# Gathers of both MoE layers in groups of four, with the landing of each group awaited at the next border

## The reference

```
h = layernorm(x) * (1 + ca) + sa;   x = x + ga * attention(h)
h = layernorm(x) * (1 + cb) + sb;   x = x + gb * ffn(h)
```

```
gate, up = split(routed_in @ gate_up);  routed = (up * silu(gate)) @ down
shared = silu(h @ Wg.T) * (h @ Wu.T) @ Wd.T;   ffn = shared + routed
```

## Time and profile before

| what | value |
| --- | --- |
| times of three runs | 1258.29, 1261.92, 1263.23 us |
| profiled execution, its own time | 1255.22 us |
| its span | 1253.4 us |
| PE busy | 1061.6 us, 85% of the span |
| DVE busy | 938.9 us, 75% |
| ACT busy | 780.5 us, 62% |
| POOL busy | 323.2 us, 26% |
| mean granted TensorE clock | 0.926 of full speed |

### The profile page before, as it was taken

The page is one execution under the profiler, slowest core; times in us unless marked ns, Lnnn a source line. Parts: engine busy times, 40 slices in busy tenths (PEclk is TensorE's granted clock), DMA queues, the critical chain, the costliest instruction groups (busy, mean ns, idle before and its releaser), DMA issues. The chain is left out here.

```text
span 1253.4 us, 23783 instructions
## 1 busy us (share of the span) xinstructions
PE 1061.6 (85%) x9052; PEld 507.1 (40%) x9052; DVE 938.9 (75%) x1445; ACT 780.5 (62%) x1539; POOL 323.2 (26%) x464
## 2 busy tenths in 40 slices
PE   6886789577779999999999999999998997179737
PEld 4785689433302222222222222222222974157315
DVE  7976244477799999999999999999990873046216
ACT  4544233144408999999999999999999452025101
POOL 4632548566410000000000000000000707700630
PEclk9998889798958999999999999999999988579959
DMA  7011466249960122112222201212000071211212
GB/s 225 1 35 35 122 169 182 90 55 209 235 116 2 33 32 32 22 14 33 32 33 33 32 6 29 33 32 33 2 3 2 12 186 45 53 30 60 59 33 59
DMA packets 94439, 76.92 MB, mean 61 GB/s; under 512 B 43220, under 2 KB 73300, under 8 KB 93816
## 3 DMA queue, kind: packets, MB, share of 16 engines
q1 hardware_dynamic: 89464, 65.42, 23.3%
q0 software_dynamic: 4864, 10.00, 3.5%
HBM read 47.77 MB, written 27.54 MB: 60 GB/s over the span
## 5 line engine op out<-in xcount | busy, mean ns | idle before, releaser
L1465 DVE TENSOR_REDUCE mx<-p_psA 128x1 f32<-128x1024 f32 x512 | 585.1, 1216 | 8.4 <-PE p_psA L1628 8.4
L1556 ACT ACTIVATE p_pt<-p_psS 128x512 f32<-128x512 f32 x1024 | 548.1, 596 | 36.8 <-PE p_psS L1650 17.1
L1663 PE MATMUL p_acc<-p_pt,V 128*32 128x256 f32 x4096 | 327.9, 392 | 15.4 <-ACT attn L1547 13.8
L1628 PE MATMUL p_psA<-K,Q 48*128 48x512 bf16 x1024 | 319.3, 394 | 9.4 <-DVE mx L1465 7.8
L1650 PE MATMUL p_psS<-Q,K 51*128 51x512 bf16 x1024 | 309.5, 384 | 0.0
L1663 PEld LDWEIGHTS p_acc<-p_pt,V 128*32 128x32 f32 x4096 | 81.8, 108 | 210.6 <-ACT p_pt L1556 110.5
L1628 PEld LDWEIGHTS p_psA<-K,Q 48*128 48x128 bf16 x1024 | 57.0, 94 | 232.3 <-DVE mx L1465 198.3
L1382 POOL TENSOR_TENSOR mr<-zeros,mx 128x16 f32<-128x16 f32 x32 | 7.1, 223 | 545.8 <-DVE mx L1465 545.8
L1932 DVE TENSOR_TENSOR f_part<-f_bank,mod 128x512 f32<-128x512 f32 x7 | 4.8, 692 | 97.9 <-remote 89.3
L1650 PEld LDWEIGHTS p_psS<-Q,K 51*128 51x128 bf16 x1024 | 62.6, 93 | 18.1 <-ACT p_pt L1556 12.6
L1894 PE MATMUL f_bank<-wsd,f_m 128*128 128x128 f32 x224 | 34.1, 295 | 41.1 <-issue 41.1
(11 more groups left out here) (343 smaller groups left out, 1474.4 us busy)
## 6 DMA issues: line engine op xcount, KB each, us to landing
f_w<-in_w SPq DMA_DIRECT2D x40, 256.0 KB
Q<-q_rows SPq DMA_DIRECT2D x32, 192.0 KB, 4.8
K<-k_rows SPq DMA_DIRECT2D x32, 192.0 KB, 5.3
result<-f_shared_kept SPq DMA_DIRECT2D x11, 256.0 KB, 2.3
result<-f_y SPq DMA_DIRECT2D x10, 256.0 KB
V<-v_rows SPq DMA_DIRECT2D x16, 144.0 KB, 5.7
hrows<-h SPq DMA_DIRECT2D x4, 516.0 KB, 7.7
x<-in_x SPq DMA_DIRECT2D x4, 512.0 KB, 5.5
```

The source lines that it names most:

```text
L1465: dve.tensor_reduce(mx[v % 2][:, h, qt:qt + 1], psA[t][:], AX.X, ALU.max).then_inc(a_max, 1)
L1556: act.activation(pt[s % 2][:, head_at(s, j), :], psS[k % 3][:], ACT.Exp, scale=INV_SCALE).then_inc(s_out, 1)
L1628: mm = pe.matmul(psA[t][:, c * 512:(c + 1) * 512], Q[g % NBUF][rows, pair, q0:q0 + P], K[g % NBUF][rows, pair, c * 512:(c + 1) * 512], sta ...
L1663: mm = pe.matmul(acc[VW * h:VW * (h + 1), cols], V[g % NBUF][:, kc, h * (HD + 1):h * (HD + 1) + VW], pt[s % 2][:, h, cols], start=(kc == 0 ...
```

## The change

A constant `LANDED = 1` takes the place of `WINDOW = 3` in layer 1's last phase, for both series of gathers: each group now waits for the landing of the group just before it, and the rings of semaphores shrink from four to two. In layer 0's experts POOL waits for the landing of the previous group at every border instead of at each second one; the waits for transposes stay. Sizes, order and number of the gathers are the same, and no other engine's code changes except for the length of the rings it indexes.

```diff
 WINDOW = 3
+LANDED = 1
@@ phase_ffn0, gpsimd
                     if k % GT == 0:
-                        if q >= 2 and q % 2 == 0:
+                        if q == 1:
+                            for s in first:
+                                pool.wait_ge(s, 16)
+                        elif q >= 2:
                             pool.wait_ge(got[q - 1], 16 * GT)
                         if q == WINDOW:
                             pool.wait_ge(x0_T, GT)
@@ phase_ffn1
-        got = [n.sem(f"got{i}") for i in range(WINDOW + 1)]
+        got = [n.sem(f"got{i}") for i in range(LANDED + 1)]
...
-        gathered = [n.sem(f"gathered{i}") for i in range(WINDOW + 1)]
+        gathered = [n.sem(f"gathered{i}") for i in range(LANDED + 1)]
@@ phase_ffn1, gpsimd, gathers of the experts
-                    if k % GT == 0 and q >= WINDOW:
-                        pool.wait_ge(got[(q - WINDOW) % len(got)], 16 * GT * ((q - WINDOW) // len(got) + 1))
+                    if k % GT == 0 and q >= LANDED:
+                        pool.wait_ge(got[(q - LANDED) % len(got)], 16 * GT * ((q - LANDED) // len(got) + 1))
@@ phase_ffn1, gpsimd, gathers of the results
-                    if i % 4 == 0 and c >= WINDOW:
-                        pool.wait_ge(gathered[(c - WINDOW) % len(gathered)], 64 * ((c - WINDOW) // len(gathered) + 1))
+                    if i % 4 == 0 and c >= LANDED:
+                        pool.wait_ge(gathered[(c - LANDED) % len(gathered)], 64 * ((c - LANDED) // len(gathered) + 1))
```

## The result

The changed kernel took **1193.14 us** (median of 4 runs, 1189.14 to 1194.74) against 1262.24 us of the kernel before beside it (4 runs): a ratio of 0.9454, 95% interval 0.9429 to 0.9479. The profiled execution took 1194.49 us, its span 1192.6, at a mean granted clock of 0.95 (0.926 before).

The account below looks back on a forecast made before the run. Long unbroken gather series were taken to hold PE's signals, idling PE 37 and 30 us. Savings of 41.6 + 27.7 + 1 = 70.3 us from 1255.2 gave 1184.9; with 6.7 us to the median, 1191 us, range 1176 to 1248.

Parts of the forecast that it names:

- the mechanism forecast first: Layer 1's last phase: long unbroken gather series stop PE's signals, borders cure it fully; 1191 us, chance 0.64.
- The sum: Whole kernel: 41.6 + 27.7 + 1 = 70.3 us off the profiled execution's 1255.2 us, giving 1184.9.
- Experts: Layer 1's experts: last copy ends at 1120.3 instead of 1161.9, so -41.6 us.
- Last phase: From the experts' last copy to the last add: 60.8 us instead of 88.5, so -27.7 us.
- Layer 0: Layer 0's experts: new waits cost at most about 1.5 us, up to 5 us of held signals may go; -1 us taken.
- What a border costs: POOL idles 1.93 us instead of 0.30 at each border: +1.63 us, bounds +1.47 and +1.88; a group's period becomes 6.63 us.
- From the last landing to the last copy: End of layer 1's experts: 3.7 us taken, against 4.4 us from last transposition to last copy in a full pipe.
- Bound by the gathers: Layer 1's experts: from about group 7 on, the gathers set the stage's pace; groups wanted 4.2 us apart or later.
- The shared expert's side of the last phase: Last phase: the shared expert's work alone would end 58.3 us after the stage's start, against 60.8 by the gathers.
- The distance of median and profile: Whole kernel: the median was 6.7 us above the profiled execution, and the same distance was expected of the new kernel.
- (a): Rival: signals held within each group, coming out only at borders; median 1246 us, or 1219 at three quarters progress; chance 0.22.
- (b): Slower rival: the stop ends only after a series' last landing, so borders only add 29 us; 1291 us, chance 0.10.

Follow-up runs that it names:

- the parts alone: Kernel before with only layer 1's experts' gathers, only the results' gathers, or only layer 0 changed: 1226.56, 1237.92 and 1257.34 us.
- the depth of two: Kernel before, both layer 1 series waiting for the landing of the group before the last one, layer 0 as before: 1263.01 us, ratio 1.0001.
- chip 9: Changed kernel, unaltered, against the kernel before on a chip where that takes 1163.1 us: 1192.86 us, ratio 1.024.

## Why the prediction was right, and where it was not

The time predicted was 1191 us, the time measured 1193.14, and the mechanism forecast first is the one that the parts alone and the depth of two show: the stop comes with the unbroken series, in each series by itself, and a border after four gathers keeps it away there. What holds the signals stays unknown, and that 1191 lies within 3 us of the measured time is luck in part: the profiled execution was forecast at 1184.9 us and took 1194.49. Point by point:

- **The sum.** 70.3 us predicted, 69.1 by the medians. Experts: -37.5 instead of -41.6 with the same start (the part alone: -36.7). Last phase: -24.3 instead of -27.7 (alone: -25.4). Layer 0: -5.3 at the projections' first gather instead of -1 (alone: -5.9). Three terms are off by 3.4 to 4.3 us, and the last offsets part of the others.
- **What a border costs.** 1.93 us of idle was taken. The usual one is shorter, 1.78 to 1.88, but four are longer, 2.26 to 4.07. Group 11 began at 1112.92, not 1110.3: 1.04 of that is the later start of the series, the rest these longer pauses. The bound of 1.88 us added per border was too tight for single ones; the trace of before had a 2.18, but nothing like 4.07. (The 43 gathers from 1042.42 to 1096.33 are 44, with 43 intervals; the 1.25 us stand.)
- **From the last landing to the last copy.** 3.7 us was taken, below the 4.4 us that a full pipe takes from the last transposition. The last tile is transposed at 1120.99 and copied by 1125.43: 4.4 us. No row allowed going below. The other part is that the last transposition itself comes about 1.8 us after its tile's landing (issued at 1112.92 + 3 x 1.25 = 1116.67, landed 2.5 us later), since the tiles before it are in the pipe.
- **Bound by the gathers.** Right for the end of both stages: the last groups' rows are awaited by PE, and in the last phase by DVE for 6.15 us. But PE waits for rows only from group 9 on, not from 7, since its own loop is slower there than the 4.2 us a group of the forecast: from group 2 on its transpositions of four tiles come 4.8 to 5.8 us apart, with no wait for rows. The changed kernel on the chip without stops has 4.22 us between them and waits from group 6 on. So with borders the stopping chip still delays PE's chain a little within a group; the gathers' pace covers it. PE's timeline of the result, then of the changed kernel without stops:

```profile
1072.80 0.63 PE L2317 MATMUL f_bank<-ident,h 128*128 128x128 f32 x4
1078.64 0.63 PE L2317 MATMUL f_bank<-ident,h 128*128 128x128 f32 x4
...
1105.50 0.66 PE L2317 MATMUL f_bank<-ident,f_shared_kept 128*128 128x128 f32 x4 [1.67 <-DMA f_shared_kept<-hrows,gidx]
1112.71 0.66 PE L2317 MATMUL f_bank<-ident,f_shared_kept 128*128 128x128 f32 x4 [3.02 <-DMA f_shared_kept<-hrows,gidx]
```

```profile
1075.71 0.63 PE L2317 MATMUL f_bank<-ident,h 128*128 128x128 f32 x4
1079.93 0.63 PE L2317 MATMUL f_bank<-ident,h 128*128 128x128 f32 x4
1085.74 0.66 PE L2317 MATMUL f_bank<-ident,h 128*128 128x128 f32 x4 [1.66 <-DMA h<-hrows,gidx]
```

The shared expert's side of the last phase, put at 58.3 us, is 57.1 on the chip without stops; the gathers' side, put at 60.8, is 64.2, of which 2.2 us are the one long pause of 4.07.

- **Layer 0.** The step "nearer to nothing, because signals were held there even within a group of four" was wrong. Where signals are held the borders bring 5.3 to 5.9 us. Where they are not, they cost 10 to 16 (15.2 on the chip that ran the change; five traces with these borders against three without), not at most 1.5: I counted only the border at group 1 as felt, and took the wait for transposes to hide those from group 5 on. That wait of 5.26 us goes with the late signals: POOL's waits for transposes sum to 16 us or more in the four traces with stops that have the old layer 0, and to under 1 us in the three without. POOL's waits for landings in layer 0 without stops, the kernel before and then the changed one (us in all, times, longest):

```profile
POOL h L987 <- DMA h<-hrows,gidx: 8.3, 3, 3.1
...
POOL f_spare L987 <- DMA h<-hrows,gidx: 3.3, 1, 3.3
...
POOL h L987 <- PE f_bank L1124: 0.6, 2, 0.3
```

```profile
POOL h L991 <- DMA h<-hrows,gidx: 20.5, 7, 4.5
...
POOL f_spare L991 <- DMA f_spare<-hrows,gidx: 3.5, 1, 3.5
POOL f_spare L991 <- DMA h<-hrows,gidx: 3.3, 1, 3.3
```

The wait for transposes is 0.6 us there and hides nothing; nine borders wait 27.3 us, four waited 11.6. The difference, 15.7 us, is about the stage's loss. In the result POOL waits for landings there only 17.5 us (and 2.3 us for transposes); why less on that chip no row tells.
- **The distance of median and profile.** 6.7 us was carried over; the profiled execution after was 1.4 us above its median. Profile to profile the change is 60.7 us, not 70.3: a distance that did not hold, +6.7 instead of -1.4, brought the forecast of the median 8 us nearer. The middle stretch, which the change does not touch, was 6.4 us longer in that execution, within the 801.3 to 809.6 us that it takes in the traces of the table.
- **The rivals.** (a), held within each group: not as a whole, since the two lines have no wait on "remote" and the time is far from 1246 and 1219; in part yes, by the short waits on "remote" and the slower loop above, which the traces without stops don't have. (b), tied to the series as a whole: the mechanism falls, and its premise, that both stops end only after the last landing, does not hold for the first chunk's signal of 1059.41. But its side of zero is what chip 9 shows, by a cause that I had not among the rivals: no stop at all. "What holds the signals no row shows" was the place where this rival belonged. I took a stop that one chip's trace showed for a property of the kernel.

The rule of the Trainium skill that I weighed ("SBUF — State Buffer", section "SBUF: two separate sides", that DMA and engines have ports of their own and so don't slow each other) describes the chips with 1163 to 1165 us: PE is busy 44.40 of 48 us beside 38 gathers, at 97 GB/s. Where the kernel before takes 1262 us, PE and the gathers are not independent: signals are 29.6 us late in the last phase, and PE crawls beside 53 GB/s in the first series. The section speaks of ports, and nothing shows that ports are what is short there.

**What stays open.** Why one chip stops and three don't: no row tells, and chip and session can't be told apart, since each chip ran one set. One thing beside the times differs. The six traces taken where the kernel before stops hold 5264 to 5506 records of semaphore updates by DMAs, the eight others 7176 to 7191, for the same number of transfers; what is missing lies in the stretches in which indirect gathers run. So on that chip either several updates arrive as one, or some are not recorded. Each of these executions was itself recorded, and that the recording takes part in the stop is a rival that no run tests. Whether the cure is the pause or the landing, and whether series of eight or sixteen are short enough there. For eight speaks that the first signals held in layer 1 are those of about 14 and 15 us after the first gather (the last prompt ones came after about 11 and 12), longer than eight gathers take (10 us); against it, that layer 0 had borders each eight gathers and late signals all the same. For sixteen (20 us) nothing speaks. Borders each eight in layer 1's two series with layer 0 left as before would, by the table, cost 7.2 us without stops; that kernel was not run, and none that was run beats both: of those run the kernel before is the best on three chips, by 1.0% or more, and the changed kernel where it stops, by 33 us over the best of its parts.

## What to carry to other kernels

When a trace shows engines released together, tens of us after the work they wait for, find out on a second chip whether the stop is there before paying for its cure: the same edit was worth -5.5% on one chip and +2.4% on another. A wait that is to break a series must really wait (here depth one did, depth two never), and it is free only as often as the stage has slack: here each sixteen gathers cost nothing, each eight 7 us, each four 19. And a wait read from a disturbed trace must not be counted as cover for a new one, since it may go with the disturbance.

## What the runs showed of the hardware

The same program at the same intervals of POOL took 1255 to 1267 us where it stops and 1160 to 1169 us on three other chips, with granted clocks of 0.915 to 0.926 and 0.951 to 0.959 as the mean. The lower clock follows the stop: in the kernel before it is 1.00 in the first 14 us of the series, still 0.99 when PE is busy only 0.91 of 3 us, and 0.50 after that:

```profile
1053.00:1056.00 3.00, 0.91 (x5) 0.59 (x4) 0.00 (x0) 0.00 (x0) 2.26 (x3) 0.99 0.22 48
...
1060.00:1070.00 10.00, 1.86 (x5) 1.55 (x6) 3.25 (x6) 0.00 (x0) 7.62 (x8) 0.50 0.23 53
```

Gathers went on at one per 1.25 us through both stops, and their landings were seen, since POOL waits for none in the kernel before. DVE and ACT had no signal under way in the last phase's stop, so whether theirs would be held is not shown. With gathers broken after four, the long stops are gone in layer 1, and delays of 1 to 4 us are left.
